# Both rotary products of a step in one VectorE instruction, and the clamp of the square sums on GpSimd

## The reference

```python
qkv = x @ Wqkv                       # 128 -> 3 * 1024
q = l2norm(q) * qs                   # t / max(norm(t), 1e-12)
k = l2norm(k) * ksc
q = q * cos * scale + rotate_half(q) * sin * scale
k = k * cos * inv + rotate_half(k) * sin * inv
out = local_attention(q, k, v)       # each window sees itself and the one before
x = out @ Wo + x                     # then the feed-forward
```

## Time and profile before

| | |
|---|---|
| median of three runs | 2322.53 us |
| profiled execution | 2319.96 us |
| its span, first to last instruction | 2318.0 us |
| TensorE busy | 1991.3 us (86%) |
| VectorE busy | 1698.9 us (73%) |
| ScalarE busy | 1470.9 us (63%) |
| GpSimd busy | 1239.8 us (53%) |
| VectorE, clamp L1094 | 384 times, mean 0.420 us |
| VectorE, products L1106 and L1108 | 384 times each, mean 0.681 and 0.677 us |

### The profile page before, as it was taken

One profiled execution on the slowest core, in us unless ns is written; L12 is line 12 of the kernel. 1 busy time (PEld: TensorE's weight loads), 2 busy tenths in 40 slices (PEclk: granted clock), 3 DMA queues, 4 the chain that ended last, 5 costly groups with the idle time before them and its releaser, 6 DMA issues. The chain is left out here.

```text
span 2318.0 us, 85232 instructions
## 1 busy us (share of the span) xinstructions
PE 1991.3 (86%) x32884; PEld 1450.5 (63%) x32884; DVE 1698.9 (73%) x3114; ACT 1470.9 (63%) x4554; POOL 1239.8 (53%) x1362
## 2 busy tenths in 40 slices
PE   4546566499989999999999999999999999999997
PEld 2212122398677697676876867857769768687672
DVE  6579897598587696775876867858669677686673
ACT  2443232397677696676767867767669667686772
POOL 3046664576475375574554854647537557455450
PEclk7779899699999999999999999999999999999998
DMA  1022120411112111121111221111211111111110
GB/s 35 3 81 72 63 72 0 146 41 41 32 42 72 38 42 37 36 79 31 43 37 31 51 70 36 40 32 42 71 38 42 37 36 43 32 44 29 25 31 18
DMA packets 147573, 103.90 MB, mean 45 GB/s; under 512 B 15778, under 2 KB 140256, under 8 KB 145504
## 3 DMA queue, kind: packets, MB, share of 16 engines
q1 hardware_dynamic: 147184, 98.55, 15.3%
HBM read 47.79 MB, written 1.18 MB: 21 GB/s over the span
## 5 line engine op out<-in xcount | busy, mean ns | idle before, releaser
L947 ACT ACTIVATE PR<-ps,MN 128x64 f32<-128x64 f32 x1536 | 354.9, 313 | 389.3 <-DVE MN L1069 388.8
L1198 POOL TENSOR_TENSOR QK<-PC,PS 128x256 f32<-128x256 f32 x384 | 278.6, 725 | 600.1 <-DVE PS L1108 543.0
L1203 POOL TENSOR_TENSOR QK<-QK,RN 128x512 f32<-128x512 f32 x384 | 401.6, 1046 | 161.1 <-ACT RN L937 133.0
L821 PE MATMUL ps<-W,XS 128*128 128x256 f32 x1536 | 399.3, 383 | 19.2 <-DMA W<-in_Wqkv 18.9
L793 PE MATMUL ps<-V,PT 64*32 64x65 f32 x12288 | 301.7, 220 | 8.6 <-ACT PT L988 5.1
L821 PEld LDWEIGHTS ps<-W,XS 128*128 128x128 f32 x1536 | 264.4, 192 | 41.4 <-DMA W<-in_Wqkv 20.5
L807 PE MATMUL ps<-ident,QK 128*128 128x128 f32 x1536 | 253.2, 287 | 35.8 <-POOL QK L1203 33.5
L1199 POOL TENSOR_TENSOR QK<-PC,PS 128x256 f32<-128x256 f32 x384 | 278.9, 726 | 0.0
L1092 DVE TENSOR_REDUCE SS<-SQ 128x8 f32<-128x512 f32 x384 | 259.3, 675 | 16.4 <-ACT SQ L979 16.4
L793 PEld LDWEIGHTS ps<-V,PT 64*32 64x32 f32 x12288 | 257.4, 105 | 18.7 <-ACT PT L988 9.2
L1069 DVE TENSOR_REDUCE MN<-ps 128x4 f32<-128x256 f32 x384 | 161.1, 419 | 142.2 <-PE ps L774 140.0
(11 more groups left out here) (142 smaller groups left out, 3447.4 us busy)
## 6 DMA issues: line engine op xcount, KB each, us to landing
V<-V SPq DMA_DIRECT2D x384, 97.5 KB, 2.2
scr<-B_rows SPq DMA_DIRECT2D x32, 512.0 KB, 3.6
V<-V SPq DMA_DIRECT2D x288, 32.5 KB, 1.9
W<-in_Wqkv SPq DMA_DIRECT2D x48, 192.0 KB, 2.9
TC<-in_tcos SPq DMA_DIRECT2D x6, 1024.0 KB, 5.9
TS<-in_tsin SPq DMA_DIRECT2D x6, 1024.0 KB, 8.4
WO<-in_Wo SPq DMA_DIRECT2D x6, 512.0 KB, 4.7
W<-in_W SPq DMA_DIRECT2D x6, 341.0 KB, 3.4
```

Of the source, the lines that this page charges most:

```text
L821: mm = nc.tensor.matmul(ps[:, par, k * 2 * P:(k + 1) * 2 * P], cols[k], W[:, i, 0:2, :].rearrange("p t m -> p (t m)"), start=True, stop=True)
L947: e = nc.scalar.activation(PR[:, m % 2, h, slot * DH:(slot + 1) * DH], ps[:, 4 + h, slot * DH:(slot + 1) * DH], ACT.Exp, scale=-1.0, bias= ...
L1198: nc.gpsimd.tensor_tensor(QK[:, par, :, 0:hd], PC[:, par, :, 0:hd], PS[:, par, :, hd:DH], ALU.add)
L1203: nc.gpsimd.tensor_tensor(QK[:, par, :, :], QK[:, par, :, :], bcast_last(RN[:, par, :], DH), ALU.mult).then_inc(qk, 1)
```

## The change

The two tables become halves of one tile TCS, and the two products halves of one tile PCS. The names TC, TS, PC and PS stay as views of them, so loads, scalings and the adds are as before. VectorE forms both products with one instruction of 1024 columns. Its first input is the 512 columns in PSUM, read twice through a repeated axis; its second is the pair of tables. The semaphore prods is raised once, as before. The clamp is no longer a VectorE instruction against LEAST, but a tensor_scalar on GpSimd, the first thing in rotate: GpSimd waits for the square sums (ss), clamps, raises ssm, and only then waits for the products. LEAST, its memset and VectorE's wait for it are gone. The diff is whole but for the declaration of the semaphore s_least:

```diff
-        TC = sb("TC", [P, 2, L // P, 2 * P])
-        TS = sb("TS", [P, 2, L // P, 2 * P])
+        TCS = sb("TCS", [P, 2, 2, L // P, 2 * P])
+        TC, TS = TCS[:, :, 0], TCS[:, :, 1]
         lnb = sb("lnb", [P, 1])
-        LEAST = sb("LEAST", [P, 8])
...
-        PC = sb("PC", [P, 2, 8, DH])
-        PS = sb("PS", [P, 2, 8, DH])
+        PCS = sb("PCS", [P, 2, 2, 8, DH])
+        PC, PS = PCS[:, :, 0], PCS[:, :, 1]
...
         @block.vector
         def _(dve):
-            dve.wait_ge(s_least, 1)
-
...
                 nc.vector.tensor_reduce(SS[:, m % 2, :], SQ[:, m % 2, :, :], AX.X, ALU.add).then_inc(ss, 1)
-                dve.wait_ge(ss, m + 1)
-                nc.vector.tensor_tensor(SS[:, m % 2, :], SS[:, m % 2, :], LEAST[:], ALU.max).then_inc(ssm, 1)
...
-                src = ps[:, par, :].rearrange("p (k c) -> p k c", k=2)
-                nc.vector.tensor_tensor(PC[:, par, :, :].rearrange("p (k a) d -> p k (a d)", k=2), src,
-                                        TC[:, l % 2, 2 * s:2 * s + 2, :], ALU.mult)
-                nc.vector.tensor_tensor(PS[:, par, :, :].rearrange("p (k a) d -> p k (a d)", k=2), src,
-                                        TS[:, l % 2, 2 * s:2 * s + 2, :], ALU.mult).then_inc(prods, 1)
+                both = TCS[:, l % 2, :, 2 * s:2 * s + 2, :].rearrange("p t k c -> p t (k c)")
+                nc.vector.tensor_tensor(PCS[:, par, :, :, :].rearrange("p t a d -> p t (a d)"),
+                                        ps[:, par, :].unsqueeze(1).to_broadcast([P, 2, CH]), both, ALU.mult).then_inc(prods, 1)
...
-            nc.gpsimd.memset(LEAST[:], 1e-24).then_inc(s_least, 1)
...
+                par, hd = m % 2, DH // 2
+                pool.wait_ge(ss, m + 1)
+                nc.gpsimd.tensor_scalar(SS[:, par, :], SS[:, par, :], 1e-24, None, ALU.max).then_inc(ssm, 1)
                 pool.wait_ge(prods, m + 1)
                 wait(pool, qkT_ps, m - 1)
-                par, hd = m % 2, DH // 2
```

More of the change, by code:

```diff
@@ L634, in transformer_block @@
         stored = [sem("stored%d" % c) for c in range(NCH)]
-        s_vz, s_ones, s_v0, s_half, s_lnb, s_least = (
-            sem(k) for k in ("s_vz", "s_ones", "s_v0", "s_half", "s_lnb", "s_least"))
+        s_vz, s_ones, s_v0, s_half, s_lnb = (
+            sem(k) for k in ("s_vz", "s_ones", "s_v0", "s_half", "s_lnb"))
         qkv_dram = d["Wqkv"].rearrange("l p (t i m) -> l p i t m", t=3, i=PAIRS)
```

## The result

The changed kernel takes 2324.28 us in the median (2320.14 to 2329.18 over 20 runs), the kernel before 2321.07 us in as many runs beside it. The ratio is 1.0017, with a 95% interval of 1.0009 to 1.0025: 3.9 us slower, between 2.1 and 5.8. The forecast was 2328 us, 6 us more than before; the sign is right, and the size lies just above the interval.

What follows compares the result with a forecast made beforehand. TensorE was taken to bound ordinary steps at 3.45 us, GpSimd the table steps. Losses of 4.7 (tables), 2.6 (feed-forwards) and 0.2 (start) less 1.5 (slow intervals) made 6.0 us more: forecast 2328 us, range 2314 to 2339.

Steps and rivals of the forecast that it cites:

- Ordinary steps are TensorE's: Loop of 384 steps: an ordinary step repeats at 3.45 us on TensorE without idle, so VectorE savings there are hidden.
- The 44 slow intervals: Loop intervals of about 3.49 us where VectorE's stretched clamp is late; removing it gains 44 x 0.034 = 1.5 us.
- the sum: Whole kernel: 4.7 tables + 2.6 feed-forwards + 0.2 start - 1.5 slow intervals = 6.0 us longer.
- The product: VectorE's merged multiply of 1024 columns: 1.207 us like L473 instead of 1.28 for the pair, saving 0.07 a step.
- The clamp's price: GpSimd's tensor_scalar of 8 columns: taken as 0.19 us, between bounds of 0.094 and 0.291.
- c: Time the clamp adds to GpSimd's queue: 0.15 us, between 0.05 and 0.25.
- The rival at twice VectorE's price: GpSimd's clamp takes 0.33 us, giving 2336; chance 0.25, shared with ScalarE's wait being larger than worked out.
- Feed-forward, 3c - 0.21: Before 11 feed-forwards, three clamps in GpSimd's line delay ScalarE's last logarithm: 0.24 us each, 2.6 us.
- Table stretches, 0.34 + 4c: Five stretches where GpSimd scales the next layer's tables: ScalarE waits for the clamp, 0.94 us each, 4.7 us.
- The chain from a logarithm's start to the end of the copy of P: ScalarE's work in a table step, with nothing to wait for: 3.14 us.
- the earlier start of GpSimd's adds: Table steps: without VectorE's clamp the products end earlier, so GpSimd's first adds may start 0.92 us earlier.
- -2.05 + 54c: Whole kernel's change in us as a formula of the clamp's share of GpSimd's queue; its ends give +0.7 and +11.5.

Runs made afterwards that it cites:

- product_only: Changed kernel with the clamp back on VectorE against LEAST, the product still merged; ratio to the kernel before 0.9991 (0.9981 to 1.0001).
- clamp_twice: Changed kernel with a second, useless 8-column tensor_scalar in front of GpSimd's clamp; ratio to the kernel before 1.0073.
- clamp_early: Changed kernel with GpSimd's clamp moved right behind the multiply, ahead of table scaling and affine pair; ratio to the kernel before 1.0007.
- clamp_only: Kernel before with its two products kept apart and only the clamp moved to GpSimd, first in rotate; ratio to the kernel before 1.0029.
- dve_scalar_clamp: Merged product with the clamp on VectorE, as one-input tensor_scalar instead of two-input tensor_tensor; ratio to the kernel before 0.9987.
- no_clamp_bias: Changed kernel with no clamp instruction; ScalarE's logarithm adds 1e-24 through its bias; 2308.80 us, ratio to the kernel before 0.9953.

## Why the prediction was right, and where its sizes were off

**Ordinary steps are TensorE's.** Right. They stay at 3.45 us in all kernels, in the changed one with VectorE 166 us emptier. The 44 slow intervals went (one left): 1.5 us, as in the sum. That the clamp alone made them late is too simple: 40 of them went in product_only, with the clamp still on VectorE.

**The product.** Right: 1.215 against 1.207 worked out, hidden.

**The clamp's price.** Too low: 0.233 us against 0.19, c = 0.20 against 0.15. It lies inside the bounds. The rival at twice VectorE's price (0.33) fell: 1.40 times VectorE's undisturbed 0.166. The 1.96 times of the Trainium skill, GPSIMD Engine Reference, section 3.1, agrees with L544 against L473 (1.98) and not with this instruction of 8 columns.

**Feed-forward, 3c - 0.21.** With the measured c it is 0.39; measured +0.36, eleven times: 4.0 us (2.6 in the sum). clamp_twice confirms the slope and clamp_early that the three clamps in GpSimd's line are its cause.

**Table stretches, 0.34 + 4c.** With the measured c it would be 1.14; an undisturbed stretch lost 0.75. The chain from a logarithm's start to the end of the copy of P was mis-sized. The 3.14 us were read where ScalarE ran close behind its inputs: from the start of the squares to that of the copy of P it is 0.62 us there. After ScalarE has been held for 2 us the same two starts are 0.49 apart, and the chain is 1601.12 - 1598.25 = 2.87 us. That is 0.27 of the missing 0.39. Most of the rest is the earlier start of GpSimd's adds: it was reckoned at 0.92 us, and without a clamp a stretch gained 1.01 to 1.03 (0.04 of it the slow interval that stands in each).

**What was not foreseen: TensorE's clock.** In one table stretch of the changed kernel's first trace 2.45 us were lost, not 0.75. By windows of time (us from the start of the span, then the busy time of PE, PEld, DVE, ACT and POOL with their instructions, the granted clock, the DMA share and GB/s):

```profile
1920.00:1925.00 5.00, 3.76 (x82) 2.99 (x82) 2.76 (x5) 2.97 (x12) 4.92 (x7) 1.00 0.11 27
1926.00:1927.00 1.00, 0.74 (x45) 0.55 (x33) 0.42 (x1) 0.97 (x6) 1.00 (x3) 1.00 0.08 16
1927.00:1928.00 1.00, 1.00 (x9) 0.93 (x6) 0.88 (x3) 1.00 (x7) 0.92 (x2) 0.64 0.07 16
1928.00:1929.00 1.00, 1.00 (x4) 0.81 (x3) 1.00 (x2) 0.58 (x2) 0.79 (x2) 0.50 0.47 111
...
1931.00:1932.00 1.00, 1.00 (x67) 0.92 (x64) 0.27 (x1) 0.87 (x4) 0.00 (x0) 1.00 0.00 0
```

TensorE had waited for ScalarE in four loaded steps and worked 3.76 of the 5 us from 1920 to 1925. Then the granted clock fell, just after 1927, from 1.00 to 0.50, that is from 2.4 to 1.2 GHz, during the projections, and was at 1.00 again at 1931. The same projections take 1.92 us instead of 1.03:

```profile
1926.95 0.84 PE L806 MATMUL ps<-ident,QK 128*128 128x128 f32 x4
1927.59 1.92 PE L820 MATMUL ps<-W,XS 128*128 128x256 f32 x4
...
1932.57 1.03 PE L820 MATMUL ps<-W,XS 128*128 128x256 f32 x4
```

Of the 25 table stretches in the traces of the five kernels that keep their pieces of 1024 columns and have a clamp on GpSimd (changed twice, clamp_only, clamp_twice, clamp_early), 12 have a fall of the clock inside. 6 of these lose 1.4 to 1.7 us more than their neighbours, the other 6 at most 0.1. Of the 25 stretches in before (twice), product_only, dve_scalar_clamp and no_clamp_bias, none has one. Loaded steps take about 5.15 us or more there and at most 4.97 here. That the longer steps cause the falls is what the counts suggest; no run isolates it.

**The sum.** In the traces the named terms come to 3.9 (tables) + 4.0 (feed-forwards) + 0.4 (start) - 1.2 (slow intervals outside the tables) = 7.1 us without a fall of the clock, and the two pairs of traces differ by 5.6 and 10.5 us in the span. The timed runs give 3.9 (2.1 to 5.8). Why they give about 3 us less is open: the start of the first projection (436.1 us in before, 438.0 in the changed kernel, ahead of all that was changed), the loads at u = 4 and 5 (up to 3 us) and the tail vary by as much from one execution to the next. So each part of the 6.0 was right to within 1.5 us, and the total owes something to luck: the tables were put 0.8 us too high and the feed-forwards 1.4 too low. With the measured c the prediction's own formula, -2.05 + 54c, gives 8.8 us; the price taken too low and the chain taken too long offset each other. Against the timed runs 6.0 is somewhat high.

## What to carry to other kernels

A small instruction moved to an idle engine costs where that engine's queue is full, not where it is idle: look for the longest block that can stand ahead of it in the new queue, and for who waits in order behind its result. Put it ahead of such a block if its input is there by then, or spread the block. Where the queue is full its own price (0.20 us here) is paid in each step as well. Best here was to fold it into an instruction that exists, the logarithm, as its bias (0.9953 against 1.0017). And of two edits that come together, time each alone: here the clamp alone lost 0.3%, and the product alone lost nothing (0.9991).

## What the runs showed of the hardware that I had not expected

- A VectorE tensor_scalar of 8 columns with a constant is held by GpSimd as the two-input form is: 171 to 1042 ns, over 240 ns in 201 of 384.
- GpSimd's tensor_scalar of 8 columns takes 225 to 258 ns in all kernels that have it, and where work is queued behind it the next instruction starts 0.20 us after its own start.
- A logarithm of 8 columns on ScalarE takes 321 ns in the mean with a bias column and 239 without (the shortest 300 and 208).
- TensorE's granted clock fell to half in 12 of 25 table stretches with loaded steps of about 5.15 us or more, and in none of 25 with 4.95.
